# Layer 0's scores and maxima on half arrays with packed queries, and experts that begin on five full tiles of the first three batches

## The reference: what is computed

```python
# layer 0: 16 heads of 16 features, keys = 512 context rows + 512 tokens
x = x + tanh(g_xattn[0]) * L0_attention(layernorm(x), ctx)
#   attn = softmax(einsum('bhnd,bhmd->bhnm', q * scale, k)); out = attn @ v; out @ w_proj.T + b
x = x + tanh(g_ffn[0]) * L0_ffn(layernorm(x))
# layer 1: 16 heads of 64 features, a null key and value, a layernorm with scale and bias on the output
x = x + tanh(g_xattn[1]) * L1_attention(layernorm(x), ctx)
# layer 1's experts: X = layernorm(x), 8 experts, the 2 best of each token, weights w = softmax of their logits
logits = X @ Wg + bg
topv, topi = top_k(logits, 2);  w = softmax(topv)
xs = X[:, None] * w[..., None]
y_e = (silu(xs @ W1[e]) * (xs @ W3[e])) @ W2[e]      # H = 1024, for the experts e in topi only
x = x + tanh(g_ffn[1]) * (X + sum of the two y_e)
```

## Time and profile before

| | before |
|---|---|
| median of 3 runs | 2034.28 us (2030.84 to 2037.16) |
| the profiled execution | 2036.09 us |
| its span, first to last instruction | 2034.4 us |
| PE busy | 1792.8 us, 88% of the span |
| DVE, ACT, POOL busy | 1181.5, 1116.2, 423.8 us |
| mean granted TensorE clock | 0.947 of full |

### The profile page before, as it was taken

One profiled execution on the slowest core, in us unless ns is written; L12 is line 12 of the kernel. 1 busy time (PEld: TensorE's weight loads), 2 busy tenths in 40 slices (PEclk: granted clock), 3 DMA queues, 4 the chain that ended last, 5 costly groups with the idle time before them and its releaser, 6 DMA issues. The chain is left out here.

```text
span 2034.4 us, 28113 instructions
## 1 busy us (share of the span) xinstructions
PE 1792.8 (88%) x9516; PEld 1121.3 (55%) x9516; DVE 1181.5 (58%) x2893; ACT 1116.2 (55%) x2334; POOL 423.8 (21%) x430
## 2 busy tenths in 40 slices
PE   5899998998996599999999999999982599999994
PEld 3455554554543234444444444445442599999994
DVE  4868768767772455545564465435644455555554
ACT  2566666666674155544554455445550467777662
POOL 3101200200201100000000002000202377766762
PEclk9999999999998699999999999899986799999997
DMA  3000000000000770000000001000001766666644
GB/s 94 1 21 1 21 1 1 22 1 1 1 1 0 263 245 1 21 1 0 1 21 1 0 1 43 1 0 1 23 1 51 249 212 202 203 208 214 217 152 140
DMA packets 122862, 134.13 MB, mean 66 GB/s; under 512 B 9248, under 2 KB 116640, under 8 KB 122720
## 3 DMA queue, kind: packets, MB, share of 16 engines
q1 hardware_dynamic: 115696, 119.45, 18.6%
q0 software_dynamic: 3744, 10.49, 1.4%
q10 hardware_dynamic: 3280, 2.40, 0.4%
HBM read 101.63 MB, written 30.69 MB: 65 GB/s over the span
## 5 line engine op out<-in xcount | busy, mean ns | idle before, releaser
L622 DVE TENSOR_REDUCE l_tile_max<-psum 128x1 f32<-128x512 f32 x512 | 341.8, 688 | 108.1 <-PE psum L345 106.7
L483 ACT ACTIVATE l_probs<-psum 128x1024 f32<-128x1024 f32 x256 | 248.3, 1022 | 99.3 <-PE psum L357 95.7
L345 PE MATMUL psum<-l_kT,l_qT 128*128 128x512 f32 x512 | 236.2, 469 | 40.9 <-DVE l_tile_max L622 37.6
L2013 POOL TENSOR_TENSOR moe_w_lo<-moe_w,moe_w_hi 128x512 fp32r<-128x512 f32 x179 | 233.2, 1303 | 139.6 <-ACT moe_w_hi L1886 138.9
L1380 DVE TENSOR_REDUCE l_row_max<-psum 128x2 f32<-128x1024 f32 x128 | 156.4, 1222 | 182.1 <-PE psum L1000 181.3
L1210 ACT ACTIVATE l_null_p<-l_s_null,l_neg_max 128x1 f32<-128x1 f32 x256 | 73.9, 289 | 285.2 <-DVE l_neg_max L1382 285.2
L1846 PE MATMUL psum<-moe_xs_hi,moe_w_hi 128*128 128x256 f32 x736 | 211.3, 287 | 1.4 <-DVE moe_xs_lo L1923 1.4
L1846 PE MATMUL psum<-moe_xs_lo,moe_w_hi 128*128 128x256 f32 x736 | 209.3, 284 | 0.0
L1846 PE MATMUL psum<-moe_xs_hi,moe_w_lo 128*128 128x256 f32 x736 | 209.3, 284 | 0.0
L1986 DVE TENSOR_TENSOR psum<-psum,moe_gate 128x256 f32<-128x256 f32 x184 | 79.3, 431 | 166.1 <-ACT moe_gate L1900 166.1
L1212 ACT ACTIVATE l_probs<-psum,l_neg_max 128x512 f32<-128x512 f32 x256 | 171.5, 670 | 0.0
(11 more groups left out here) (238 smaller groups left out, 3246.8 us busy)
## 6 DMA issues: line engine op xcount, KB each, us to landing
moe_w<-in_moe_w SPq DMA_DIRECT2D x276, 256.0 KB, 4.4
moe_sorted_x<-l_zeros SPq DMA_DIRECT2D x1, 17680.0 KB, 57.1
moe_xs<-moe_sorted_x SPq DMA_DIRECT2D x23, 272.0 KB, 2.9
l_ctxT<-in_ctxT SPq DMA_DIRECT2D x4, 1024.0 KB, 5.4
x_resid<-in_x SPq DMA_DIRECT2D x4, 512.0 KB, 10.1
l_raw<-in_ctx SPq DMA_DIRECT2D x4, 512.0 KB, 3.5
l_v_raw<-in_ctx SPq DMA_DIRECT2D x4, 512.0 KB, 3.6
l_wk<-in_wkv SPq DMA_DIRECT2D x1, 2048.0 KB, 16.1
```

The lines of the kernel that those rows point to most:

```text
L345: nc.tensor.matmul(bank(max_bank(m)), qT[:, q % SLOTS, h, t * P:(t + 1) * P], kT[:, q % SLOTS, h // 2, half * BANK:(half + 1) * BANK], sta ...
L483: nc.scalar.activation(probs[:, n % PT_RING], wide(2 * (n % 2)), ACT.Exp, scale=SCALE).then_inc(exp_done, 1)
L622: nc.vector.reduce_max(tile_max[:, q % 2, t, h, half:half + 1], bank(max_bank(m)), AX_X).then_inc(max_read, 1)
L2013: nc.gpsimd.tensor_tensor(w13_lo[:, k % SPLITS], w13[:, slot_k, :, cols], w13_hi[:, k % SPLITS].bitcast(F32), ALU.subtract).then_inc(w13_s ...
```

## The change

**Layer 0.** `qT` becomes half as wide: two heads lie one above the other, as in `kT`. `max_scores` and `scores` take only the 64 rows of their head (`rows_of`), so each uses half of the array's rows, and the two score matmuls of a pair use different halves. A "q" fill is read with one activation of 128x512. The clearing of `qT` goes.

```diff
-        qT = sb("qT", [P, SLOTS, HQ, N], F32R)
+        qT = sb("qT", [P, SLOTS, HQ // 2, N], F32R)
+        def rows_of(h):
+            return slice((h % 2) * ST, (h % 2 + 1) * ST)
...
-                    nc.tensor.matmul(bank(max_bank(m)), qT[:, q % SLOTS, h, t * P:(t + 1) * P],
-                                     kT[:, q % SLOTS, h // 2, half * BANK:(half + 1) * BANK],
+                    nc.tensor.matmul(bank(max_bank(m)), qT[rows_of(h), q % SLOTS, h // 2, t * P:(t + 1) * P],
+                                     kT[rows_of(h), q % SLOTS, h // 2, half * BANK:(half + 1) * BANK],
                                      start=True, stop=True).then_inc(max_psum, 1)
...
                     for i in range(2):
-                        last = nc.tensor.matmul(bank(2 * (n % 2) + i), kT[:, q % SLOTS, c, kt * P:(kt + 1) * P],
-                                                qT[:, q % SLOTS, 2 * c + i, :], start=True, stop=True)
+                        last = nc.tensor.matmul(bank(2 * (n % 2) + i), kT[rows_of(i), q % SLOTS, c, kt * P:(kt + 1) * P],
+                                                qT[rows_of(i), q % SLOTS, c, :], start=True, stop=True)
...
-                        for i in range(2):
-                            rows = slice(i * ST, (i + 1) * ST)
-                            last = nc.scalar.activation(qT[rows, x % SLOTS, 2 * y + i, :], src[rows, :], ACT.Copy)
+                        last = nc.scalar.activation(qT[:, x % SLOTS, y, :], src, ACT.Copy)
...
-                nc.gpsimd.memset(max_cols[:], 0.0)
-                nc.gpsimd.memset(qT[:].bitcast(F32), 0.0).then_inc(filled, 1)
+                nc.gpsimd.memset(max_cols[:], 0.0).then_inc(filled, 1)
```

```diff
+        self.FIRST = -(-(TOP * (self.T - self.TT) * P - self.E * (ROWS - 1)) // ROWS)
...
                     if b + 1 == s.B:
                         c = b - 1
+                        if at == (6, 0):
+                            rank_experts()
+                        if at == (6, 1):
+                            router.compare_tops(dve).then_inc(tops, 1)
+                        if at == (6, 2):
+                            dve.wait_ge(scattered, 16 * TOP * T * c)
+                            router.choose_slots(dve).then_inc(slots_ready, 1)
                         if at == (6, 3):
-                            rank_experts()
+                            dve.wait_ge(exped, c + 1)
+                            router.weigh_tops(dve).then_inc(weights_ready, 1)
+                            add_residual(c, range(T))
                         if at == (7, 0):
-                            compare_tops()
+                            router.count_tiles(dve, ROUTED * T, ROWS - 1)
                         if at == (7, 1):
-                            weigh_tops(c)
-                            add_residual(c, range(T))
+                            router.sum_tiles(dve)
+                            note_used()
                         if at == (7, 2):
-                            choose_slots(c)
+                            router.list_experts(dve, 0, s.FIRST)
+                        if at == (7, 3):
+                            router.list_starts(dve, 0, s.FIRST)
+                            router.end_starts(0, s.FIRST)
...
+        CHAIN = {"rT": 10, "logits": 12, "counts": 17, "exp": 17, "scale": 21, "scatter": 22}
```

SP no longer waits for the table before the first tile, but before tile 5, and the rows of tile 5 come behind all its weights:

```diff
-                sp.wait_ge(tiles_ready, 1)
+                sp.wait_ge(scattered, 16 * TOP * TB * LAST_B)
+                load_rows(0)
                 for m in range(PIECES):
-                    if m == W_SLOTS:
-                        sp.wait_ge(scattered, 16 * TOP * T)
-                        load_rows(0)
-                        load_rows(1)
                     i, part = divmod(m * PIECE, FT)
                     if part == 0:
+                        if i == FIRST:
+                            sp.wait_ge(tiles_ready, 1)
                         e = sp.value_load(expert_ids[0:1, i:i + 1], min_val=0, max_val=E - 1)
-                        if m >= W_SLOTS:
+                        if i >= 2 and i != FIRST:
                             load_rows(i)
                     load_weights(m)
+                    if m == 1:
+                        load_rows(1)
+                    if i == FIRST and part == FT - PIECE:
+                        sp.wait_ge(scattered, 16 * TOP * T)
+                        load_rows(FIRST)
```

More of the change, by code:

```diff
@@ L90, in statistics_steps, with fine_steps, refine @@
         yield
+    def fine_steps(self, dve, rows, eps):
+        nc, n = self.nc, self.tiles
+        var, guess, half, tmp = (self.work[:, i, 0:n] for i in range(4))
+        dve.drain()
+        for t in range(n):
+            nc.vector.bn_stats(self.stats[:, t, :], rows(t))
+        yield
+        dve.drain()
+        for t in range(n):
+            nc.vector.bn_aggr(self.mv[:, t, :], self.stats[:, t, :])
+        dve.drain()
+        nc.vector.tensor_scalar(var, self.mv[:, 0:n, 1], 1.0, eps, ALU.mult, ALU.add)
+        yield
+        dve.drain()
+        nc.vector.tensor_scalar(tmp.bitcast(U32), var.bitcast(U32), 1, None, ALU.logical_shift_right)
+        nc.vector.tensor_scalar(half, var, -0.5, None, ALU.mult)
+        dve.drain()
+        nc.vector.tensor_scalar(guess.bitcast(U32), tmp.bitcast(U32), -1.0, float(RSQRT_MAGIC), ALU.mult, ALU.add)
+        dve.drain()
+        self.refine(dve)
+        yield
+        for _ in range(self.STEPS - 1):
+            self.refine(dve)
+        yield
+    def refine(self, dve):
+        nc, n = self.nc, self.tiles
+        _, guess, half, tmp = (self.work[:, i, 0:n] for i in range(4))
+        nc.vector.tensor_tensor(tmp, guess, guess, ALU.mult)
+        dve.drain()
+        nc.vector.tensor_tensor(tmp, tmp, half, ALU.mult)
+        dve.drain()
+        nc.vector.scalar_tensor_tensor(out=guess, in0=tmp, scalar=1.5, in1=guess, op0=ALU.add, op1=ALU.mult)
+        dve.drain()
     def apply(self, out, row, t):
@@ new lines, in add_output, with add_residual @@
+                def add_output(some):
+                    for t in some:
+                        last = nc.vector.scalar_tensor_tensor(out=last_tokens[:, t, :], in0=rows[:, t, :],
+                                                              scalar=norm_out.work[:, 1, t:t + 1], in1=last_tokens[:, t, :],
+                                                              op0=ALU.mult, op1=ALU.add)
+                    return last
+                def add_residual(some):
+                    for t in some:
+                        nc.vector.scalar_tensor_tensor(out=last_tokens[:, t, :], in0=routed[:, t, :], scalar=g["gates"][:, 3:4],
+                                                       in1=last_tokens[:, t, :], op0=ALU.mult, op1=ALU.add)
@@ L1943, in list_tiles, with scale_rows, join_tables @@
+                def scale_rows(some):
+                    for t in some:
+                        nc.vector.tensor_scalar(router.rows[1][:, t, 0:D], routed[:, t, :], router.weight[:, 1, t:t + 1], None,
+                                                ALU.mult).then_inc(scaled_dve, 1)
+                def join_tables():
                     dve.drain()
[L1944 to L1945 removed]
+                    nc.vector.tensor_tensor(router.n_tiles[:], router.n_tiles[:], router.used[:, 0:E], ALU.subtract)
+                    nc.vector.tensor_tensor(router.unused[:], router.used[:, 1:E + 1], router.used[:, 0:E], ALU.subtract)
@@ new lines, in add_first_used @@
+                def add_first_used():
+                    some = slice(FIRST, TILES)
+                    nc.vector.scalar_tensor_tensor(out=router.tile_start[:, some],
+                                                   in0=router.used[:, 0:1].to_broadcast([P, TILES - FIRST]), scalar=float(ROWS),
+                                                   in1=router.tile_start[:, some], op0=ALU.mult, op1=ALU.add)
+                    dve.drain()
+                first, second = range(0, TB // 2), range(TB // 2, TB)
@@ new lines, in _ @@
+                dve.wait_ge(g["out_psum"], TB)
+                for _ in norm_out.statistics_steps(dve, lambda t: bank(t)[:, 0:D], LN_OUT_EPS):
+                    pass
+                split_down(0)
+                split_rows(0)
+                for t in range(TB):
+                    last = nc.vector.scalar_tensor_tensor(out=rows[:, t, :], in0=bank(t)[:, 0:D],
+                                                          scalar=norm_out.mv[:, t, 0:1], in1=g["ln_scale"][:],
+                                                          op0=ALU.subtract, op1=ALU.mult)
@@ L1982, in _ @@
+                last.then_inc(out_read, 1)
+                for k in range(1, AHEAD):
+                    split_down(k)
                 for k in range(STEPS + 1):
@@ L2027, in store_results @@
                         in_=y_sb[:, i % 2, h, :], in_offset=None).then_inc(y_stored[i % 2], 16)
+                for k in range(AHEAD):
+                    split_up(k)
+                pool.wait_ge(scattered, 16 * TOP * TB * LAST_B)
```

(3 more changed lines are left out.)

563 lines of the change are left out of this document (346 added, 217 removed).

## The result

The changed kernel took 2068.96 us (median of 4, 2061.06 to 2073.4) against 2035.72 us (median of 4, 2030.84 to 2043.08); the ratio is 1.0156, with a 95% interval of 1.0112 to 1.02. The forecast was 1975, with a range of 1941 to 2006: wrong in its sign. The profiled execution's span is 2067.3 us, 32.9 more than before.

The account below looks back on a forecast made before the run. PE was taken to lead layer 0, though not alone, and to be busy throughout the experts. −51.8 + 3.4 + 1.3 + 0.9 + 3 − 5 − 10.8 = −59.0 took the profiled 2036.1 to 1977.1; forecast 1975 us, range 1941 to 2006.

Parts of the forecast that it names:

- The seam: Layer 1's last projection to the first `up` matmul: 63.2 us shrinks to a chain of 11.4, saving 51.8.
- Layer 0, the matmuls: Layer 0's paired scores save 53.8 us, shape changes around fills cost 45.6 at 0.17 each: net gain 8.2.
- Layer 0, the waits: Layer 0: 0.7 of the net 8.2 counted because PE waits for DVE in 35 places: −5.7 us.
- The first 84 us: Layer 0's terms for one ACT copy per "q" fill, −4 us, and for no clearing of `qT`, −1.1.
- The clearing's term: Ahead of layer 0's first queries: without the `qT` clearing a small DVE operation takes about 0.17 instead of 1.30, −1.1 us.
- End of layer 1: PE's 3.57 us wait behind batch 2's ranks goes, with part of a low-clock stretch: −5, bounds −8 and 0.
- What moves into the experts: Experts' steps: PE's routing matmuls +3.4 us, ACT's exponential and table loads +1.3, DVE +0.9, rows of tile 5 +3.
- the rows of tile 5: Experts: SP issues these rows only after the table and four weight pieces, so PE waits: +3 us, bounds 0 to 6.
- DVE idles 1.07 ... it fits: Experts' steps: up to 2.5 us more DVE work fits in most steps' idle time and slack, not step 29: +0.9.
- DVE ahead of its first step: Seam: DVE's output statistics, a fifth of 29.2 us, end while the first weights land: no cost.
- R3: Rival, layer 0: each shape change costs 0.34 us, so layer 0 +21 and 2007 in all; 17 in 100.
- R5: Rival, layer 0: half-array matmuls don't run side by side, weight loads lie open, pitch 0.33, about 2088; 3 in 100.

Follow-up runs that it names:

- b1: Changed kernel with layer 0 of before, POOL clearing the low-half buffer instead of subtracting for the first 39 expert steps: 2000.32 us against 2032.03, ratio 0.9841.
- f2: Kernel before plus 80 unread rounded-f32 matmuls behind layer 1, alternating 64 rows and whole array: 79 distances of 0.42 or 0.43 us; one execution.
- a1 to a3: Kernel before with, in layer 0, only scores on half arrays, only maxima, or the change's whole layer 0: 2060.34, 2161.55 and 2089.93 us against 2036.39.
- f1 to f3: Kernel before plus 80 unread rounded-f32 matmuls behind layer 1: 64 rows, alternating, or whole array; 0.23 us apart, 0.42 or 0.43, and 0.23.

## Why the prediction was wrong, point by point

- **The seam** ("saved: 63.2 − 11.4 = 51.8"): right, 10.35 and 52.9. It ended on POOL's split, as said. But DVE's part ahead of it was as late: in b1, where POOL clears in 0.53, the same stretch is 10.95 and ends on DVE's low half of the rows.
- **Layer 0, the matmuls** ("Net 8.2"): right in kind, and better than forecast. Pairs start together, and the work at full clock fell by 16. A change costs 0.20 by itself (f2) where I had 0.17, and a fill's way in and out +0.35 where I had 0.34.
- **Layer 0, the waits** ("of which I count 0.7"): the step that failed first. A 0.7 lets waits hide a part of a gain; here they grew by more than the gain. The maxima go through two banks, and DVE needs 0.69 for each; matmuls that come closer together meet the same DVE. PE's waits for it rose from 34.7 to 53.9, its time without a matmul by 24. A kernel with more banks for the maxima was not run.
- **Layer 0, the clock:** the step that failed most, for the forecast had no term for it. PE was at the low clock for 10 us of the steps in the kernel before and for 86 in the changed one. At half speed the 76 more are worth up to 38 us, the largest term of the 46; had the clock stayed, some of it would have come back as waits for DVE. That it hangs together with half arrays is shown by a1 to a3; by which property isn't (above). Together: −16 + 24 + 38 = +46, where the forecast had −5.7, and −4 for the copy.
- **The first 84 us** ("−4" and "−1.1" for copy and clearing): first values at 84.5 instead of 74.0. The clock up to them is 0.72, in the kernel before it was 0.91: low from 47.3 to 88.3 in one piece. The clearing's term was right in itself, the operation of 1.30 now takes 0.17, but the input landed 0.76 later, and DVE's norm starts 0.38 earlier and not 1.1. For the copy no run shows a gain; PE's waits for it were 3.0 in all in before (L418 and L436), so 4 was more than there was.
- **End of layer 1** ("−5"): +1.7, outside the bound of 0. The wait at the ranks went, and three of 1.8, 1.5 and 3.3 came. They stand where DVE does batch 2's tops, slots, and weights with the addition to the residual, and not at the table, as the reason given with the bound had it. The longest ends at 1565.15, behind that addition (1562.16, 1.67 long) and ahead of the table's first operation (1565.19):

```profile
1565.15 1.09 PE L1320 MATMUL psum<-ident,l_probs 128*128 128x128 f32 x8 [3.34 <-DVE l_probs L1560]
```

- **What moves into the experts** ("+3.4", "+1.3", "+0.9", "+3", in all +8.6): +27.7. PE's routing matmuls and the rows of tile 5 (0.6 instead of 3) were no worse than said. The step that failed is "DVE idles 1.07 ... it fits". It took the length of DVE's operations from a place where POOL didn't run beside them. DVE idles just while POOL subtracts (in before DVE from 1675.51 to 1676.58, POOL's row from 1675.56 to 1676.85). PE waited 17.3 us, 4.3 of it in the gap of the next point, and three times long enough for 3.4 us at the low clock behind it (5 us more). With the 3.4 of the routing matmuls that is 26 of the 27.7; the rest I can't place.
- **DVE ahead of its first step:** "that ends under the landing: no cost". True of the statistics. But four low halves, an addition and a table load stand between the first `up` and the first `down`, and in before they lay under the 17 us in which SP fetched eight pieces. That cover went with the seam: 4.3.
- **The rivals:** none had the mechanism. R3's 0.34 a change is 0.20 (f2), and its +21 for layer 0 fell short. R5, the slower one, decided from 48 lost in layer 0, and layer 0 lost 56.5; but it blamed half arrays that don't run side by side and exposed weight loads, and the step shows pairs side by side. Its nearness is luck.

## What to carry to other kernels

A faster matmul in a loop that shares its banks with another engine is worth what that engine lets through. Packing on half arrays has to be counted in the order of the program, since each change to another shape costs nearly as much (0.20) as a pair saves (0.23): scores or maxima alone cost work, both together saved 16 us. And a sum of matmul times isn't yet a forecast: those 16 stood against 24 of new time without a matmul and 38 of lower clock, so read the granted clock of the loop first. When work is moved into another engine's idle time, look who runs in that idle time: an operation of 0.17 beside POOL's subtraction took 1.78. And when a wait goes, list all that it had covered, down to the low halves that nobody had to wait for.

## What the runs showed of the hardware that I had not expected

- Between a half-array and a whole-array matmul 0.43 pass, between two of one shape 0.23 (f1 to f3, 80 matmuls each), whichever way round.
- Two half-array matmuls on different halves start within 0.01 of each other, even when one is a maximum and the other a score, and their weights are different.
- A DVE operation of 8 columns with two inputs took 1782 ns beside POOL's subtraction and 166 inside POOL's clearing of the same buffer. One with a single input and 4 columns took 1.30 us beside a clearing (before, L74 of the earlier trace rows: it ends at 9.86, the clearing at 9.84), and 0.17 without one (changed kernel).
- 34 us of matmuls that alternate between shapes, and 29 us on one half of the array, kept the full clock of 2.4 GHz, though the same kinds of matmul in layer 0 ran at a mean of 0.93.
